# Four graph-attention layers on one core: the last layer's softmax maximum taken in two parts, its first eight row tiles prepared during the dense rounds

## The reference

```python
h = tanh(input @ W + b)
inp = input @ W
e = (h @ a)[:, 0]                       # one score for each row j
valid = sum(h, axis=1) != 0
mask = (adj > 0) & valid[None, :]
m = max(where(mask, e[None, :], neg), axis=1)
w = where(mask, exp(e - m), 0)
att = w / max(sum(w, axis=1), 1e-30)
return att @ inp
```

## Time and profile before

| | us |
|---|---|
| median of 3 runs | 2999.37 (2997.71 to 3000.24) |
| the profiled execution | 2995.74 |
| its span | 2993.9 |
| TensorE busy | 2923.0 (98%) |
| VectorE busy | 2133.9 (71%) |
| ScalarE busy | 1920.6 (64%) |
| GpSimd busy | 1179.6 (39%) |

### The profile page before, as it was taken

The page is one execution under the profiler, slowest core; times in us unless marked ns, Lnnn a source line. Parts: engine busy times, 40 slices in busy tenths (PEclk is TensorE's granted clock), DMA queues, the critical chain, the costliest instruction groups (busy, mean ns, idle before and its releaser), DMA issues.

```text
span 2993.9 us, 65253 instructions
## 1 busy us (share of the span) xinstructions
PE 2923.0 (98%) x24628; PEld 2556.9 (85%) x24628; DVE 2133.9 (71%) x3887; ACT 1920.6 (64%) x3414; POOL 1179.6 (39%) x1559
## 2 busy tenths in 40 slices
PE   7999999999989999999999999999999999989999
PEld 6899999999979999999998878887788878755555
DVE  5999898888888888888896556566666656562245
ACT  4777999999988999999985545444455444430000
POOL 0672385641226565654121023333323333444222
PEclk9999999999999999999999999999999999999999
DMA  8677100000100000000010000000000000000001
GB/s 292 207 234 246 39 11 15 11 11 14 62 15 13 11 15 11 15 11 15 11 35 12 4 1 4 4 1 4 1 4 4 1 1 1 3 1 1 0 14 42
DMA packets 41912, 104.55 MB, mean 35 GB/s; under 512 B 9856, under 2 KB 23424, under 8 KB 33536
## 3 DMA queue, kind: packets, MB, share of 16 engines
q1 hardware_dynamic: 39616, 101.61, 10.4%
q10 hardware_dynamic: 2112, 0.52, 0.1%
HBM read 97.73 MB, written 4.39 MB: 34 GB/s over the span
## 4 chain that ended last, share of the span: by engine, by line
PE 89%; DVE 5%; ACT 2%; issue 2%; DMA 1%; POOL 1%; SPq 0%; DVEq 0%; POOLq 0%; ACTq 0%
PE bank L1377 21%; PE bank L1380 21%; PE bank L1435 16%; PE bank L1473 13%; PE bank L1383 11%; PE bank L1308 2%; PE bank L1462 2%; DMA arena<-in_adj_dram 1%; PE bank L1449 1%; DVE rings L1804 1%; DVE arena L1724 1%; PE bank L1320 1%; ACT above L974 1%; PE bank L1358 1%; DVE rings L1799 1%
## 5 line engine op out<-in xcount | busy, mean ns | idle before, releaser
L1377 PE MATMUL bank<-values,rings 128*128 128x195 bf16 x8192 | 1392.1, 248 | 31.5 <-DVE rings L1807 19.0
L1380 PE MATMUL bank<-values,rings 128*128 128x195 bf16 x8192 | 1392.0, 248 | 0.0
L974 ACT ACTIVATE above<-srow,kpass 128x512 fp8e4<-128x512 f32 x2032 | 1279.9, 709 | 96.2 <-DVE rings L1807 87.1
L1377 PEld LDWEIGHTS bank<-values,rings 128*128 128x128 fp8e4 x8192 | 802.9, 98 | 44.0 <-issue 39.8
L1380 PEld LDWEIGHTS bank<-values,rings 128*128 128x128 fp8e4 x8192 | 802.9, 98 | 0.4
L1804 DVE TENSOR_TENSOR rings<-rings,above 128x512 uint32<-128x512 uint32 x512 | 387.1, 756 | 171.8 <-PE bank L1380 135.4
L1062 ACT ACTIVATE values<-srow,cmul 128x512 f32<-128x512 f32 x256 | 206.0, 815 | 411.5 <-PE bank L1473 410.5
L1807 DVE TENSOR_TENSOR rings<-rings 128x512 uint32<-128x512 uint32 x512 | 425.7, 831 | 17.3
L1473 PE MATMUL bank<-hv,values 128*128 128x257 f32 x1792 | 420.6, 380 | 0.0
L1473 PEld LDWEIGHTS bank<-hv,values 128*128 128x128 f32 x1792 | 335.0, 190 | 69.9 <-issue 25.2
L1383 PE MATMUL bank<-values,rings 128*128 128x390 bf16 x1920 | 318.7, 329 | 10.1 <-DVE values L1840 10.1
(11 more groups left out here) (223 smaller groups left out, 3483.5 us busy)
## 6 DMA issues: line engine op xcount, KB each, us to landing
arena<-in_adj_dram SPq DMA_DIRECT2D x64, 1024.0 KB, 4.9
srow<-src_dram SPq DMA_DIRECT2D x69, 256.0 KB, 3.1
x<-in_x_dram SPq DMA_DIRECT2D x4, 1024.0 KB, 11.4
out_dram<-x SPq DMA_DIRECT2D x7, 512.0 KB, 2.9
arena<-in_L_gnn_fe_w_dram SPq DMA_DIRECT2D x2, 512.0 KB, 7.2
arena<-in_L_gnn_W_hz_dram SPq DMA_DIRECT2D x1, 1024.0 KB, 7.7
arena<-in_L_gnn_g_w_dram SPq DMA_DIRECT2D x1, 1024.0 KB, 10.9
weights<-in_L_gnn_W_dram SPq DMA_DIRECT2D x3, 256.0 KB, 3.5
```

The lines of the kernel that those rows point to most:

```text
L974: last = act.activation(above[:, k % 2, q, :], srow[:, par, :], ACT.Relu, scale=BIG, bias=kpass[:, p % 2, k * Q + q:k * Q + q + 1], satura ...
L1377: pe.matmul(acc[:, 0:KW], pos[:, k % 2, q, :].bitcast(FP8)[:, rows], v[:, 0:KW], start=start, stop=final, skip_group_check=True)
L1380: last = pe.matmul(acc[:, KP:KP + KW], neg[:, k % 2, q, :].bitcast(FP8)[:, rows], v[:, KP:KP + KW], start=False, stop=final, skip_group_ch ...
```

## The change

The maximum of layer 3 becomes one in two parts. The first eight row tiles (chunk 0 of old, rounds 0 to 3 of the tanh) get a maximum of their own.

- VectorE takes it behind tanh_scores(4) (early_max), GpSimd makes it one over the partitions by a second partition_all_reduce, put between rstds(3, EG-2) and rstds(2, EG-1).
- VectorE shifts, multiplies and splits these tiles' values between the later tanh rounds (early_shift at round 8, early_mul and early_products at 10, early_cast and early_edges at 11, early_rests at 12, early_cast at 13, early_lasts at 14). Both casts are done by VectorE. The values lie in the arena, which is free by then.
- TensorE multiplies units 0 and 1 of the first group into banks 4 to 7 as soon as these values and the last h are there; units 2 to 7 go into banks 0 to 3 as before.
- VectorE sums banks 4 to 7 in units 4 and 5 of the first group, and adds them, times exp(early maximum - maximum), to the first group's sums when those are made, in unit 4 of the second group.
- The chunks of the other 24 row tiles move up: chunk u of the steps is now row tiles 8(u+1) on, and FIRST3 is laid out anew.

```diff
         def first_tiles(l, u):
...
+            if l == 3:
+                u = (u + 1) % FIRST_CHUNKS
...
                 rstds(3, EG - 2, E.l_var, E.l_rstd)
+                pool.wait_ge(E.c_pmax, 1)
+                pool.partition_all_reduce(early_top, smax[:, 0, 1:2], P, RMAX).then_inc(E.c_max, 1)
                 rstds(2, EG - 1, E.f_var, E.f_rstd)
                 finish(EG - 1)
                 rstds(3, EG - 1, E.l_var, E.l_rstd)
...
                     act.activation(emul[:, 0, 0, :], emul[:, 0, 0, :], ACT.Exp).then_inc(s_exps, 1)
+                    act.activation(early_scale, early_scale, ACT.Exp).then_inc(E.c_scale, 1)
...
                     tanh3(r)
+                    if r == 8:
+                        act.wait_ge(E.c_shift, 1)
+                        act.activation(early_exp, early_exp, ACT.Exp).then_inc(E.c_exp, 1)
...
+                early = 2 if l == 3 and first else 0
                 for k in range(BITS):
-                    if first and k % 2 == 0:
-                        pe.wait_ge(s_vfirst, first_values_before(l) + k + 2)
+                    if k < early:
+                        if k == 0:
+                            pe.wait_ge(E.c_vals, 2)
+                            pe.wait_ge(E.l_h, EG)
+                    elif first and k % 2 == 0:
+                        pe.wait_ge(s_vfirst, first_values_before(l) + k + 2 - early)
...
+                            acc = bank[GT + it if k < early else GT * par + it]
...
+                        if l == 3 and par == 1:
+                            pe.wait_ge(s_vfirst, first_values_before(3) + 2 * FIRST_CHUNKS)
...
-            FIRST3 = {0: ((first_rests, 0),),
-                      1: ((first_lasts, 0), (first_products, 1), (first_rests, 1), (first_products, 2), (first_lasts, 1)),
-                      3: ((first_rests, 2), (first_products, 3), (first_lasts, 2)),
-                      5: ((first_rests, 3), (first_lasts, 3))}
+            FIRST3 = {0: ((first_rests, 0), (first_lasts, 0)),
+                      2: ((first_products, 1), (first_rests, 1)),
+                      3: ((first_products, 2), (first_lasts, 1)),
+                      4: ((first_rests, 2),),
+                      5: ((first_products, 3), (first_lasts, 2)),
+                      6: ((first_rests, 3),),
+                      7: ((first_lasts, 3),)}
...
-                    shifted.then_inc(s_shift, 1)
+                    dve.tensor_tensor(early_scale, early_top, late_top, ALU.subtract).then_inc(s_shift, 1)
...
-                        dve.wait_ge(s_unit, unit - 1 + CREDIT)
-                        dve.tensor_scalar(edge[:, r], words, shift[0], ONE, shift[1], ALU.bitwise_and)\
-                            .then_inc(s_sides, 1)
+                        if not first or k >= UNITS_AHEAD:
+                            dve.wait_ge(s_unit, unit - 1 + CREDIT)
+                            dve.tensor_scalar(edge[:, r], words, shift[0], ONE, shift[1], ALU.bitwise_and)\
+                                .then_inc(s_sides, 1)
...
+                            if k in (4, 5):
+                                for it in (2 * k - 8, 2 * k - 7):
+                                    summed = sum_parts(3, 1, 0, it, early_sums)
+                                if k == 5:
+                                    summed.then_inc(s_sums, 1)
...
+                        if k == GT and with_early:
+                            summed.then_inc(E.c_summed, 1)
+                            dve.wait_ge(E.c_summed, 1)
+                            dve.wait_ge(E.c_scale, 1)
+                            dve.scalar_tensor_tensor(out=sums[:, 0], in0=early_sums, scalar=early_scale,
+                                                     in1=sums[:, 0], op0=ALU.mult, op1=ALU.add).then_inc(s_sums, 1)
...
+                def early_max():
+
+                    dve.wait_ge(E.l_score, CHUNK // ET)
+                    dve.tensor_reduce(smax[:, 0, 1:2], scores3[:, :, 0:CHUNK], AX.X, ALU.max).then_inc(E.c_pmax, 1)
+
+                def early_shift():
+
+                    dve.wait_ge(E.c_max, 1)
+                    dve.tensor_scalar(early_exp, scores3[:, :, 0:CHUNK], early_top, None, ALU.subtract)
+                    dve.tensor_scalar(early_valid, kscores[:, 0:1, 0:CHUNK], 0.0, None, ALU.not_equal)\
+                        .then_inc(E.c_shift, 1)
+
+                def early_mul():
+
+                    dve.wait_ge(E.c_exp, 1)
+                    dve.tensor_tensor(early_factor, early_exp, early_valid, ALU.mult).then_inc(E.c_mul, 1)
+
+                def early_products():
+
+                    dve.wait_ge(E.c_mul, 1)
+                    for vtmp, factor, columns, _ in early_tiles():
+                        dve.tensor_copy(vtmp[:, 0, :, D:C], factor)
+                        dve.tensor_tensor(vtmp[:, 0, :, 0:D], columns, factor.to_broadcast([P, CHUNK, D]), ALU.mult)\
+                            .then_inc(E.c_big, 1)
+
+                def early_cast(i):
+
+                    for kind, (vtmp, _, _, part) in enumerate(early_tiles()):
+                        dve.wait_ge((E.c_big, E.c_rest)[i], kind + 1)
+                        dve.tensor_copy(part[i], vtmp[:, i]).then_inc(E.c_cast, 1)
...
+                def early_edges():
+
+                    for k in range(UNITS_AHEAD):
+                        dve.tensor_scalar(edge[:, k], packed[:, :, 0:WORDS], 6 - k, ONE, ALU.logical_shift_left,
+                                          ALU.bitwise_and).then_inc(s_sides, 1)
...
                 tanh_scores(4)
+                early_max()
                 x_stats(EG - 2)
...
                     if r == 8:
                         x_stats(EG - 1)
+                        early_shift()
                     if r == 9:
                         x_norm(EG - 1)
+                    if r == 10:
+                        early_mul()
+                        early_products()
+                    if r == 11:
+                        early_cast(0)
+                        early_edges()
+                    if r == 12:
+                        early_rests()
+                    if r == 13:
+                        early_cast(1)
+                    if r == 14:
+                        early_lasts()
```

More of the change, by code:

```diff
@@ L396, in gnn_kernel @@
         E.l_score, E.l_inpool = sem("l3_score_made"), sem("l3_tanh_in_by_pool")
+        E.c_pmax, E.c_max, E.c_shift, E.c_exp, E.c_mul = (sem("l3_first_chunk_" + n) for n in (
+            "partition_max", "max", "shifted", "exp", "factor"))
+        E.c_big, E.c_cast, E.c_rest, E.c_vals = (sem("l3_first_chunk_values_" + n) for n in (
+            "multiplied", "cast", "rest", "made"))
+        E.c_summed, E.c_scale = sem("l3_first_group_summed"), sem("l3_first_chunk_scale")
         E.gate_in, E.gate, E.parts, E.fused, E.f_var, E.f_rstd, E.f_norm, E.x = (sem("e_out_" + n) for n in (
@@ L567, in gnn_kernel, with early_tiles @@
         edge_last = arena[:, 0:BITS * Q * WORDS].bitcast(U32).rearrange("p (k q w) -> p k q w", k=BITS, q=Q)
+        early_values = arena[:, 0:CHUNK * KP].bitcast(BF16).rearrange("p (n c) -> p n c", n=CHUNK)
+        early_exp, early_valid, early_factor = (emul[:, 1, i:i + 1, 0:CHUNK] for i in range(3))
+        early_top, late_top, early_scale = smax[:, 1, 1:2], smax[:, 1, 0:1], smax[:, 0, 2:3]
+        early_sums = srow[:, :, :].rearrange("p a i -> p (a i)")[:, 0:GT * 2 * C]\
+            .rearrange("p (t k c) -> p t k c", t=GT, k=2)
+        def early_tiles():
+            out = []
+            for kind, vtmp in enumerate((vtmp_dve, vtmp_pool)):
+                part = [early_values[:, :, kind * KW + i * C:kind * KW + (i + 1) * C] for i in range(PARTS)]
+                out.append((vtmp, early_factor.rearrange("p a n -> p n a"), h[:, 0:CHUNK, kind * D:(kind + 1) * D], part))
+            return out
         def first_tiles(l, u):
             out = []
+            if l == 3:
+                u = (u + 1) % FIRST_CHUNKS
             for kind, vtmp in enumerate((vtmp_dve, vtmp_pool)):
@@ L1370, in group @@
                     for q in range(Q):
-                        v = values[:, slot, k * Q + q, :]
-                        start, final = (k == 0 and q == 0), (k == BITS - 1 and q == Q - 1)
+                        v = early_values[:, k * Q + q, :] if k < early else values[:, slot, k * Q + q, :]
+                        start, final = (k in (0, early) and q == 0), (k in (early - 1, BITS - 1) and q == Q - 1)
                         for it in range(GT):
-                            acc = bank[GT * par + it]
+                            acc = bank[GT + it if k < early else GT * par + it]
                             rows = slice(it * P, (it + 1) * P)
@@ L1953, in stats, with sum_parts @@
                     return
-            def sum_parts(l, half, slot, it):
+            def sum_parts(l, half, slot, it, made=None):
                 step = kind_step(l)
@@ L1959, in sum_parts @@
                     .rearrange("p k (a c) -> p k c a", a=PARTS)
```

(23 more changed lines are left out.)

2 lines of the change are left out of this document (1 added, 1 removed).

## The result

| | before | after |
|---|---|---|
| median of the runs, us | 2997.96 (6 runs, 2997.21 to 3000.24) | 3011.19 (6 runs, 3007.16 to 3012.77) |
| ratio, 95% interval | | 1.0042 [1.0032, 1.0052] |
| span of the profiled execution, us | 2993.9 | 3009.2 |

The change makes the kernel 13.2 us slower. The page's first part changes as little as the sum of work does: TensorE 2.4 us more than in the earlier trace rows, VectorE 10.2 us more, for the inserts and the early sums.

A forecast was written before the change was run, and what follows sets the result against it. TensorE, busy 98% of the span, bounds the kernel; only its 10.1 us stop and 1.8 us of slow clock could be attacked. Terms sum to +13.1 us, a span of about 3007; with 3.6 for the median, 3012.5 us, range 3004 to 3019.

The forecast's parts named there:

- (a): Early all-reduce amid GpSimd's work: loading its library in and out delays VectorE and all behind it, +12.75 us.
- (b): VectorE's early work between the last tanh rounds: 7.2 us of inserts, partly filling waits, +5.9 us on the last tanh_scores.
- (c): Late all-reduce: its library is loaded in time, before the maximum, -0.85 us.
- (d): Late maximum to usable values: two edges leave, one edge and a subtraction come in, -0.24 us.
- (e): Units 0 and 1 of attention fit into TensorE's stop before the late values, -5.28 us.
- (f): TensorE's lower clock around the hand-over: half of the 1.8 us lost there is regained, -0.9 us.
- (g): Units behind unit 2: VectorE supplies values too slowly ahead of units 4 and 6, +1.7 us.
- library for free: Rival: GpSimd's code stays loaded or loads beside other work, so no change, 2999.7 us; chance 0.11.
- half of it: Rival: only one way, in or out of GpSimd's library, costs, 3006 us; chance 0.06.
- clock rival: Rival: TensorE's long stop slows its clock in the tanh rounds and first late units, up to +4, 3016.5 us; chance 0.13.
- faster: Rival: early units gain, with library free and inserts inside VectorE's waits, -8.2 us, 2991.2 us; chance 0.04.
- signs: Trace marks announced: config pairs near 2618, VectorE waiting about 13 us, 32 early matmuls, stops ahead of units 4 and 6.

The follow-up runs named there:

- e1: The changed kernel without the early all-reduce and early_max, early tiles shifted by 0 (part of the reference's maximum left out): 2995.06 us, ratio to before 0.9993.
- e2: The kernel before plus only early_max and the early all-reduce, result unused: 3010.71 us, ratio to before 1.0044.
- e5: The kernel before plus VectorE's inserts and the early maximum by TensorE and VectorE, all units and early edges left in place: 3001.77 us, ratio 1.0017.
- e3: The changed kernel with the early maximum made by a TensorE transpose and a VectorE reduction instead of GpSimd's all-reduce: 2995.72 us, ratio to before 0.9996.
- e7: The changed kernel with the four reductions of the early sums two units later (units 6 and 7): 3009.75 us, ratio to before 1.0041.
- e6: The kernel before with layer 3's late maximum made by a TensorE transpose and a VectorE reduction: 2999.21 us, ratio to before 1.0006.
- e8: The changed kernel with no maximum in layer 3 (shift 0 for both parts) and no separate early sums: 2995.59 us, ratio to before 0.9996.
- e4: e3 with the four early casts on ScalarE instead of VectorE: 2995.84 us, ratio to before 0.9994.
- e10: e3 with the early sums two units later and the inserts one tanh round sooner: 2996.28 us, ratio to before 0.9995.
- e9: e8 with early products, casts, edges, rests and lasts one tanh round sooner: 2995.32 us, ratio to before 0.9994.

## Why the prediction was right, and where its terms were off

The forecast was +13.1 us and 3012.5; the medians give +13.2 and 3011.19. On the yardstick the changed part costs 10.97, so 2 us of the agreement are luck. Term by term, from the traces of before and after:

| term | forecast | measured | from |
|---|---|---|---|
| (a) library | +12.75 | +12.41 | VectorE's first statistics behind it, 2626.81 before, 2643.55 after, less 4.32 |
| (b) inserts | +5.9 | +4.42 | from there to the late maximum, 14.64 and 19.06 |
| (c), (d) late maximum to first late unit | -1.09 | -0.65 | 6.94 and 6.29 |
| (e), (f), (g) units, clock, supply | -4.48 | -5.22 | first late unit to unit 8, 22.85 and 17.63 |
| sum | +13.1 | +10.97 | |

**(a) was right.** Its operand waited for nothing, and nothing hid the loads: 5.67 in, 0.38, 6.60 out. Removing it gave 12.0 back (e1), adding it alone 12.39 (e2). The "library for free" and "half of it" rivals fall. The Trainium skill's rule (GPSIMD Engine Reference, Instruction dispatch) would have two loads and the all-reduce at an estimated 12.3; the 12.41 of this trace lie between that and the rows' 12.75.

**(b) was too dear by 1.5 us**, by two sizes. The windows of VectorE over the stretch from its statistics to the maximum, before and after:

```profile
2626.81:2641.45 14.64, 12.38 (x41) 1.00 0.01 3
```

```profile
2643.55:2662.61 19.06, 13.33 (x65) 10.04 (x64) 18.66 (x58) 11.92 (x40) 6.80 (x8) 0.95 0.01 2
```

In the first, 12.38 is VectorE's busy time; in the second it is 18.66. So 6.28 us of work were added, not 7.2, and idle time fell from 2.26 to 0.40, so 1.86 us were filled, not 1.3. The term that was mis-sized in the work is the price of a cast: an undisturbed one goes at the edge's pace (0.42 us, 0.34 from start to start), not at 0.55, which makes 1.4 us of four in place of 2.2. The Trainium skill (VectorE: DVE Perf Modes, the perf-mode tier table) gives a copy of 4-byte numbers inside SBUF twice the rate of an operation on two tensors. The trace agrees: 0.42 us for a cast, 0.69 for the lasts of the same shape. The 6.28 is a net figure. Counted one by one, the inserts take 9.05 us from start to start, because three of them (a product, a cast, a rest) were held beside GpSimd operations, 2.9 us longer in all; the older operations of the stretch were held less, and take 9.61 us in place of 12.38. In the cover, left out 0.5 us for GpSimd's rstd and the small gaps.

**(c) was right, (d) had the wrong sign.** The late all-reduce starts 0.32 us behind the start of the maximum in place of 1.10: -0.78 (forecast -0.85). The rest of the path came out 0.13 longer in place of 0.24 shorter. Chain of waits after, then VectorE's timeline of the same stretch:

```profile
2665.00 0.66 ACT values L982
2665.68 0.71 DVE values L1868
2666.42 0.65 ACT values L982
2667.09 1.37 DVE values L1874 x2
```

```profile
2664.20 0.17 DVE L1858 COPY values<-emul 128x8 f32<-128x8 f32 x1
...
2668.38 0.42 DVE L2070 TENSOR_SCALAR rings<-packed 128x512 uint32<-128x512 uint32 x1
```

Against the earlier trace rows, it is 1.48 us from products to rests in place of 1.69, and 1.41 from rests to lasts in place of 1.55. So the two edges of 0.34 us that left the path brought 0.35 us in place of 0.68: for the other half they had stood where VectorE would have waited for ScalarE's casts, and with the edges gone the casts are on the chain. The edge of unit 2 behind the lasts took 0.41 (forecast 0.34), and the way from the all-reduce to the products grew by 0.07 (forecast 0.1). The prediction counted all the work taken away as time and did not ask what it had covered, though it asked that of its other terms.

**(e) right, (f) half of what it was, (g) right in size.** The early units left 5.28 us; e5 against e3 shows 5.08, clock and supply included. The first late unit took 4.37 us before, 1.73 more than 2.64; after, the lower clock fell inside the early units, which had room, and the whole 1.73 is gained, not 0.9. Unit 2 to unit 8 is 17.63 us, 1.79 above six units of 2.64, against the 1.7 forecast: 0.51 ahead of unit 3, 0.22 ahead of unit 4 and 1.07 ahead of unit 6 (forecast: 0.5 ahead of unit 4 and 1.2 ahead of unit 6). That VectorE's order makes the last of these, e7 shows.

**The clock rival** had its condition met, since TensorE was at 1.2 GHz for 13.6 us of the tanh rounds, but its price, up to 4 us, doesn't show: (a) and (b) came out below the forecast, and the late units ran at full clock. Where that stretch lasted 20.5 us (e7), the last scoring came 1.13 us later. The rival "faster" falls with (b): with the library gone (e3) the inserts are still on the path, and the yardstick is at -1.16, not -8.2.

**The signs.** Those announced were seen, but for one place, since a stop of 0.5 us came ahead of unit 3 and only 0.2 ahead of unit 4: the configs at 2622.3 (2618 plus the 4.3 us ahead of the mark), the 5.67 and 6.60, VectorE's wait of 12.83, fused_norm at 2636.13 (2632 forecast, plus 4.3), 32 matmuls ahead of the late ones at 2668.90 (2666 forecast, plus 4.3, less the 1.5 by which (b) was too dear), the late all-reduce 0.14 behind its operand's end.

**What stays open.** The medians and the yardstick differ, by +2.3 us for the change, +2.7 for e6, +2.4 for e8 and -1.6 for e1, and the first mark of the thirteen profiled executions lies between 2541.57 and 2547.44 us, with nothing changed ahead of it: late in the change, e6 and e8, early in e1. Whether these few us belong to the kernel's instructions or to the execution was not tried. So none of the kernels that beat the one before by 0.7 to 3.0 us on the yardstick (e1, e3, e4, e8 to e10) is shown faster by its median.

## What to carry to other kernels

Ahead of any GpSimd operation that needs another library, look for the pair of config instructions in the trace and count both ways, in and out, against what waits behind on that engine's queue; a second such operation cost 1.0 us right behind the first, while one amid ordinary work cost 12.4. A maximum across partitions has a replacement in 0.5 us of TensorE and VectorE. And before work that is taken off a path is counted as time, ask what it covered there: two edges of 0.34 us had covered part of ScalarE's casts, and their removal gained 0.35 us in place of 0.68.

## What the runs showed of the hardware that was not expected

**TensorE's clock is worth as much as these edits, and falls where it will.** The stretches at 1.2 GHz near the hand-over, us from the first mark: before, 98.6 to 108.8; e6, the same kernel up to its last maximum, 99.8 to 110.0; e8, 99.8 to 106.6; e3, only 109.0 to 112.5, though it too stood still for 3.4 us ahead of unit 0; e9, none behind 89.8. The price of a stop is what is multiplied behind it at half clock: 2.76 us in e8's early units, none in e3's, with stops of 3.75 and 3.44 us ahead; in e3 it fell on unit 2 instead, which took 4.15 us in place of 2.64. An edit that shortens a stop by half a microsecond (e6) can lose more than that again.

**A VectorE operation beside one of GpSimd can be held until that one ends.** The cast of 1.49 us started at 2651.35; GpSimd's timeline of the same kernel has a 128x512 addition of 1.33 us from 2651.23, which ends at 2652.56, and the cast ends 0.28 behind it, not much less than the 0.42 that it takes alone:

```profile
2651.23 1.33 POOL L869 TENSOR_TENSOR values<-hv,bvec 128x512 f32<-128x512 f32 x1 [2.06 <-DVE kscores L2331]
```

The Trainium skill (SBUF — State Buffer, "SBUF: two separate sides") describes a port pair that the two engines share as an exclusive lock; the rows agree. It is no cost of the change: the kernel before has it on its own operations (a score of 1.30 us at 2632.05 in place of 0.42, beside such an addition at 2631.70), and the inserts only took their turn at it.
